# A four-layer graph network on one core: where the layer 1 sums gather their slot rows, and how the node stage loads its rows

## The reference

```python
h = jnp.maximum(_layernorm(x, axis=-1), 0.0)
msum1 = segment_sum(h[src] * w[:, None], dst, n); wsum1 = segment_sum(w, dst, n)
msum2 = segment_sum(h[dst] * w[:, None], src, n); wsum2 = segment_sum(w, src, n)
neigh1, neigh2 = msum1 / wsum1, msum2 / wsum2            # 0 where the weights sum to 0
hn = jnp.concatenate([neigh1 @ W1.T, neigh2 @ W2.T], axis=1)
gi = hn @ w_ih.T + b_ih;  gh = h @ w_hh.T + b_hh
r = sigmoid(i_r + h_r);  z = sigmoid(i_z + h_z);  nn_ = tanh(i_n + r * h_n)
x = x + nn_ + z * (h - nn_)
```

## Time and profile before

| | us |
|---|---|
| median of 3 runs | 10286.35 (10271.16 to 10287.65) |
| the profiled execution | 10286.65 |
| its span, first to last instruction | 10284.9 |
| of it the start, up to 126 | 126.0 |
| of it the sums of layer 1, 126 to 3563.5 | 3437.5 |
| of it the node stage, 3563.5 to 3803.8 | 240.3 |
| of it all that follows | 6481.1 |

### The profile page before, as it was taken

One profiled execution on the slowest core, in us unless ns is written; L12 is line 12 of the kernel. 1 busy time (PEld: TensorE's weight loads), 2 busy tenths in 40 slices (PEclk: granted clock), 3 DMA queues, 4 the chain that ended last, 5 costly groups with the idle time before them and its releaser, 6 DMA issues. The chain is left out here.

```text
span 10284.9 us, 240162 instructions
## 1 busy us (share of the span) xinstructions
PE 8865.8 (86%) x58497; PEld 7104.9 (69%) x58498; DVE 5868.4 (57%) x12333; ACT 5835.7 (57%) x15502; POOL 5342.0 (52%) x5246
## 2 busy tenths in 40 slices
PE   5888888888888859999899699999998499999998
PEld 5888888888888737777566466666665376666666
DVE  6666666666666537777311455555555455555555
ACT  5666666766666535444200467767765455555555
POOL 5666666666666400000000277777775277777775
PEclk8999999999999979999899799999999799999999
DMA  3111111111111102222354344444443122222222
GB/s 120 38 36 38 36 38 36 37 37 36 38 36 37 34 21 106 112 112 112 136 190 157 122 118 118 118 118 118 118 118 97 50 73 73 73 72 72 72 73 69
DMA packets 466279, 827.25 MB, mean 80 GB/s; under 512 B 160873, under 2 KB 333102, under 8 KB 446127
## 3 DMA queue, kind: packets, MB, share of 16 engines
q0 software_dynamic: 193536, 455.41, 16.1%
q1 hardware_dynamic: 272430, 368.67, 10.4%
HBM read 672.16 MB, written 151.40 MB: 80 GB/s over the span
## 5 line engine op out<-in xcount | busy, mean ns | idle before, releaser
L1688 POOL DMA_INDIRECT x<-table,p_gidx x1632 | 1547.2, 948 | 2458.0 <-ACT p_gidx L1725 2004.0
L634 POOL DMA_INDIRECT g_G<-table,g_runs x1776 | 2061.0, 1160 | 547.5 <-issue 540.2
L2189 POOL DMA_INDIRECT c_G<-table,c_gidx x1632 | 1554.8, 953 | 505.7 <-issue 493.4
L771 PE MATMUL g_ps_cell<-g_kw,g_loh 128*128 128x98 f32 x9472 | 1280.3, 281 | 27.6 <-DVE g_kw L687 27.6
L771 PEld LDWEIGHTS g_ps_cell<-g_kw,g_loh 128*128 128x128 f32 x9472 | 1215.3, 201 | 28.0 <-DVE g_kw L687 28.0
L782 PE MATMUL g_ps_rev<-g_hrow,g_AT 128*128 128x129 f32 x7252 | 1077.5, 286 | 95.5 <-ACT g_AT L748 66.4
L1779 PE MATMUL p_ps_sum<-x 128*96 128x256 f32 x3264 | 896.6, 398 | 157.9 <-DVE hid L1714 140.7
L782 PEld LDWEIGHTS g_ps_rev<-g_hrow,g_AT 128*128 128x128 f32 x7252 | 928.2, 196 | 130.7 <-ACT g_AT L748 94.3
L804 PE MATMUL g_ps_run<-g_Gw,g_roh 128*128 128x130 f32 x3552 | 577.8, 311 | 397.6 <-ACT g_Gw L727 397.6
L1714 DVE TENSOR_TENSOR hid<-hid,p_ps_sum 96x256 f32 x1632 | 678.0, 415 | 376.6 <-DVE hid L1714 373.2
L1779 PEld LDWEIGHTS p_ps_sum<-x 128*96 128x96 f32 x3264 | 469.5, 163 | 559.2 <-DVE hid L1714 204.4
(11 more groups left out here) (346 smaller groups left out, 17417.5 us busy)
## 6 DMA issues: line engine op xcount, KB each, us to landing
adj_save<-a_A SPq DMA_DIRECT2D x74, 1568.0 KB, 5.1
a_A<-adj_save SPq DMA_DIRECT2D x74, 1568.0 KB, 6.6
c_ed<-in_edge_dram SPq DMA_DIRECT2D x1632, 25.0 KB
g_G<-table,g_runs POOLq DMA_INDIRECT x1776
x<-table,p_gidx POOLq DMA_INDIRECT x1632
p_lhs<-in_edge_dram SPq DMA_DIRECT2D x1632, 16.0 KB
c_G<-table,c_gidx POOLq DMA_INDIRECT x1632
table<-m_rows SPq DMA_DIRECT2D x17, 384.0 KB, 2.5
```

Of the source, the lines that this page charges most:

```text
L634: g.indirect_dma_start(G[:, e % GR, q, 0:D], None, table, bass.IndirectOffsetOnAxis(ap=runs[:, n % 2, 0, RQ * e + q:RQ * e + q + 1], axis= ...
L771: last = pe.matmul(ps_cell[q % 2][:, r * KEYS:(r + 1) * KEYS], loh[:, b, cell, :], kw[:, b, cell, :], start=True, stop=True)
L1688: g.indirect_dma_start(G[:, H * b + q, :], None, table2, bass.IndirectOffsetOnAxis(ap=gidx[:, b, q:q + 1], axis=0)).then_inc(gathered[b], 16)
L2189: g.indirect_dma_start(G[:, H * b + q, :], None, table, bass.IndirectOffsetOnAxis(ap=gidx[:, b, q:q + 1], axis=0)).then_inc(gathered[b], 16)
```

## The change

In the sums stage POOL's wait and the gather of hrow are moved from the head of a batch to behind the gathers of its run 3 (e == RPB - GR). In the node stage hin and xin get room for all 49 tiles instead of two chunks, each chunk a semaphore of its own, and SP issues all loads without a wait: hin 0, hin 1, xin 0, hin 2, xin 1 and so on.

```diff
                         for n in range(NBATCH):
-                            if n >= 2:
-                                g.wait_ge(rev_made, TGS * (n - 1))
-                            g.indirect_dma_start(hrow[:, n % 2, 0:D], None, table,
-                                                 bass.IndirectOffsetOnAxis(ap=dst_tab[:, n % 2, n // 2:n // 2 + 1], axis=0)).then_inc(gathered[n % 2], 16)
                             g.wait_ge(runs_in[n % 2], 16 * (n // 2 + 1))
                             for e in range(RPB):
...
+                                if e == RPB - GR:
+                                    if n >= 2:
+                                        g.wait_ge(rev_made, TGS * (n - 1))
+                                    g.indirect_dma_start(hrow[:, n % 2, 0:D], None, table,
+                                                         bass.IndirectOffsetOnAxis(ap=dst_tab[:, n % 2, n // 2:n // 2 + 1], axis=0)
+                                                         ).then_inc(gathered[n % 2], 16)
...
-                xin = sb("u_xin", [P, 2, CT, D], F32, ctx)
-                hin = sb("u_hin", [P, 2, CT, D], F32, ctx)
+                xin = sb("u_xin", [P, NTQ, D], F32, ctx)
+                hin = sb("u_hin", [P, NTQ, D], F32, ctx)
...
-                x_in = [sem(f"u_x_in{b}") for b in range(2)]
-                h_in = [sem(f"u_h_in{b}") for b in range(2)]
+                x_in = [sem(f"u_x_in{c}") for c in range(NCH)]
+                h_in = [sem(f"u_h_in{c}") for c in range(NCH)]
...
                         for c in range(NCH):
-                            if c >= 2:
-                                sp.wait_ge(turned, c - 1)
-                            sp.dma_start(hin[:, c % 2, 0:count(c), :], tiles(table)[:, tiles_in(c), :]).then_inc(h_in[c % 2], 16)
-                            if c >= 2:
-                                sp.wait_ge(added, c - 1)
-                            sp.dma_start(xin[:, c % 2, 0:count(c), :], a["x"][:, tiles_in(c), :]).then_inc(x_in[c % 2], 16)
+                            sp.dma_start(hin[:, tiles_in(c), :], tiles(table)[:, tiles_in(c), :]).then_inc(h_in[c], 16)
+                            if c >= 1:
+                                sp.dma_start(xin[:, tiles_in(c - 1), :], a["x"][:, tiles_in(c - 1), :]).then_inc(x_in[c - 1], 16)
+                        sp.dma_start(xin[:, tiles_in(NCH - 1), :], a["x"][:, tiles_in(NCH - 1), :]).then_inc(x_in[NCH - 1], 16)
...
-                            pe.wait_ge(h_in[c % 2], 16 * (c // 2 + 1))
+                            pe.wait_ge(h_in[c], 16)
...
-                                    rows = nodes[:, c % 2, k, t, :] if k < 2 else hin[:, c % 2, t, :]
+                                    rows = nodes[:, c % 2, k, t, :] if k < 2 else hin[:, CT * c + t, :]
...
-                            v.wait_ge(x_in[c % 2], 16 * (c // 2 + 1))
-                            v.tensor_tensor(x[:, tiles_in(c), :].rearrange("p t d -> p (t d)"), xin[:, c % 2, 0:count(c), :].rearrange("p t d -> p (t d)"),
+                            v.wait_ge(x_in[c], 16)
+                            v.tensor_tensor(x[:, tiles_in(c), :].rearrange("p t d -> p (t d)"), xin[:, tiles_in(c), :].rearrange("p t d -> p (t d)"),
                                             ps_back[:, 0:cols(c)], ALU.add).then_inc(added, 1)
```

## The result

The changed kernel takes **9639.31 us**, the median of 4 runs (9633.53 to 9647.66), against 10278.76 of the kernel before in the same comparison: ratio 0.9379 [0.9363, 0.9395]. Predicted were 9657, within 9600 to 9765. The profiled execution took 9633.53, its span is 9631.8.

The account below looks back on a forecast made before the run. PE was taken to bound the sums and node stages and to stay the bound. 7.41 us a batch times 72 (534 us) plus 96 us in the node stage, 630 us off 10286.65, gave 9657 us, range 9600 to 9765.

Parts of the forecast that it names:

- Part 1, the stall: Sums stage: ACT's wait for gathered slot rows, behind POOL's wait for hrow, goes: 5.42 us a batch gained.
- Part 1, the half clock: Sums stage: PE's half clock just behind the stall goes with it, 2.40 us a batch gained.
- Part 1, a third wait for AT: Sums stage, L782: PE waits for ACT three times a batch instead of two, 0.41 us a batch lost.
- POOL's room: Sums stage: POOL needs 31.1 + 8 x 0.80 = 37.5 of 38.7 us a batch, 1.2 us to spare.
- Rival 1: Sums stage: POOL becomes the bound through dearer one-hot sets; 9745 us at 1.10 us a set; chance 0.10.
- Its decision point: Sums stage: POOL's batch passes PE's 38.68 us once a one-hot set costs POOL 0.95 us.
- Its second form: Sums stage: with POOL the bound, PE's new idling also brings half clock back, 173 us more: 9918; within chance 0.10.
- Rival 2, full blocking: Sums stage: a one-hot set blocks POOL for its full length, 2.2 us and more; 10378 us, slower; chance 0.02.
- Rival 3: Sums stage: something else, run lists or a full ring, holds POOL as long; only the node stage gains, 10191 us; chance 0.03.
- Rival 4: Node stage gains nothing, its loads crowding one another or another wait taking over: 9753 us; chance 0.05.
- Part 2: Node stage: loads issued at once never wait for a chunk; 19.21 us a chunk becomes 9.6, 96 us gained.

Follow-up runs that it names:

- either part alone: Two runs of the changed kernel, each with one part put back: new sums stage with old node stage 9736.55 us, the other way round 10179.55 us.
- run 0: Not a follow-up kernel: the first group of slot rows in each batch of the sums stage, gathered by POOL, weighed by ACT and summed by PE; no time of its own.
- both float32 runs: Changed kernel with koh and the numbers it is compared with in float32 instead of bfloat16, 10177.14 us; with only the numbers in float32, 9755.34 us.

## Why the prediction was right

**Part 1, the stall: right in full.** The runs settle its cause: a wait at the head of POOL's queue, not the ring (six slots), and not the place of the node loads (either part alone). The moved wait costs POOL 0.6 us in the whole stage, hrow's new lateness costs PE nothing.

**Part 1, the half clock: right in kind, 2.40 is too much.** It was read from one batch. Of the next batch before, PE's sum of run 0 and the second cells behind it:

```profile
1561.51 2.10 PE L804 MATMUL g_ps_run<-g_Gw,g_roh 128*128 128x130 f32 x8 [5.47 <-ACT g_Gw L727]
...
1565.99 0.70 PE L771 MATMUL g_ps_cell<-g_kw,g_loh 128*128 128x98 f32 x5
```

That is 4.48 us, 1.59 over 2.89. The mean of the two batches is 2.00; over the whole stage PE is busy 149.8/72 = 2.08 us a batch less, and the filled stall gave back 1.88.

**Part 1, a third wait for AT: wrong.** I had taken off 0.41 us a batch for it. The 162 pieces and 66.4 us are the same before and after: ACT's three heavy steps delay it alike whether it idled before them or not. The two errors nearly cancel, and that is luck: 391.7/72 = 5.44 us of waiting and 2.08 of half clock make 7.52 us a batch, all of the 541.5 us, against my 5.42 + 2.40 - 0.41 = 7.41.

**POOL's room: the mis-sized term.** The account, 31.1 us and a price for each of eight sets, was right in form; a set costs 0.88 in the changed kernel, and so 0.3 to 0.4 us were left and not 1.2. The mean of 0.80 was taken from six sets of a single batch. Rival 1 didn't happen, but the extra gather, the one-hots at step 7 and both float32 runs all ran into it. Its decision point, 0.95, fits: at 0.88 PE still set the period, at 1.10 POOL did. Its second form, half clock on top, came in none of them where PE's new idling was about 1 us a piece; with pieces of up to 7.6 us, in the kernel with both in float32, the clock was 0.96.

**Rival 2, full blocking: right in kind, far too dear.** I had ruled it out by the gather beside L684, and this reading was wrong: that gather had begun first. A gather that begins inside any of the three waits for its end. But it loses only what is left of that instruction, less the 0.13 us that it gets done ahead (0.95 - 0.82), and those begun before run through, so that a set costs 0.88 us and not 2.2 or more. The koh of the first set of the earlier trace rows shows it:

```profile
1506.75 0.57 DVE L681 TENSOR_TENSOR g_koh<-key_tab,g_number 128x784 bf16<-128x784 bf16 x1
```

At the gather's start, 1506.85, 0.47 us of it are left; less 0.13 that is the 0.34 which the gather of 1.29 took more than 0.95. Even with both in float32 a set cost 1.80, under the 1.87 from which the change would have lost time; that kernel, at 45.66 us a batch, stands just under the 46.09 of before. The chance of 0.02 rested on the wrong reason.

**Rival 3**, that something else holds POOL, falls with the hrow gather alone. **Rival 4**, no gain in the node stage, falls with the loads alone.

**Part 2: right.** 9.47 us a chunk for 9.6; 97.8 us for 96. PE's idling before the transposes went from 79.7 us in 11 pieces to 4.4 in one, before the first chunk. That the cause was the queue's order I had read from two rows; the run with two buffers shows it.

## What to carry to other kernels

On a queue that works in order, a wait belongs behind everything that could go without it; look for it wherever an engine is short of rows while free slots lie behind a waiting instruction, and try the order before more buffers. Price a stall of TensorE with what the clock takes behind it, here another 2 us on 5.4, and read such a figure from more than one period, best from the engine's busy time in the whole stage. Before one row rules out a contention, look which of the two instructions began first. Before taking a wait from one engine, add up the next one's period, contention by others' instructions included: here the second engine stood 1% behind the first.

## What was not expected of the hardware

- Idling of 5.4 us in each batch brought half clock (0.93 over the stretch), 0.7 us didn't (1.00). 44 transposes of nothing in the stall gave back 136 us, 22 only 24.
- In the changed kernel each gather that POOL began well inside a VectorE instruction with two inputs in SBUF ended 0.81 to 0.83 us behind that instruction; those begun inside one with an input in PSUM took 0.94 to 0.96 us, as alone. A gather of 0.95 us took up to 2.00 us in the changed kernel and up to 4.38 with koh and number in float32.
- kw's 784 elements take 0.97 us with koh in bfloat16 and 1.59 us in float32; koh 0.57 with number in bfloat16 and 0.97 in float32. Which property of the operands of kw decides this wasn't tried.
